# Two decoder layers on one core: two places for the stacks, four pairs of exponential tiles, and the last sums tile by tile

## The chip, the cores and the metric

The kernel runs on one core of one Trainium2 chip. The metric is the device time of one execution in microseconds (us). TensorE (PE in the rows), VectorE (DVE), ScalarE (ACT), GpSimd (POOL) and SyncE (SP) each run their own list of instructions in order and wait for one another through semaphores. SyncE issues every DMA of this kernel.

## The reference

Two transformer layers in float32 on x of 4 batches x 256 tokens x 256 features. A layer is attention and then a gated feed-forward part; each adds its input back and ends in a layer norm without weights.

```python
x = layernorm(x + attn0(x))   # 32 query heads of width 8, 8 key heads
x = layernorm(x + ffn0(x))    # weights rounded to fp8 e4m3, inner width 768
x = layernorm(x + attn1(x))   # 16 query heads of width 16, 8 key heads
x = layernorm(x + ffn1(x))    # weights = lut[idx], a table of 16 values, inner width 688
# attn: softmax(q k^T / sqrt(d)) v, then Wo;  ffn: down(silu(gate(x)) * up(x))
```

The weights of ffn0 are rounded to fp8 on the chip, and those of ffn1 are looked up on the chip from integer indices.

## The kernel before, in words

The work is cut into eight **jobs**: jobs 0 to 3 are layer 0 on batches 0 to 3, jobs 4 to 7 are layer 1 on the same batches. What each engine does, and in which order, is a table `ORDER` of five long lists of step names. `max.2.0` is step `max`, job 2, unit 0; a name on several engines is that engine's share of the same step. Matters go in steps like these:

- `q.j`, `kv.j`: projections on TensorE into one of three PSUM banks FB0 to FB2, then split by ScalarE and GpSimd into three bf16 parts (`QP`, `KP`).
- `qstack.j.part`, `kstack.j.part` on SyncE: 12 DMAs for a job (6 of `QP`, 6 of `KP`) that place the parts one above the other in the **stacks** `QS` and `KS`, from which TensorE computes float32-like scores with bf16 operands. A job's stacks lie in place `j % NST`; with `NST = 3` those of job j may be written when the scores of job j-3 are computed (`score_mm`).
- `max.j.u`: four matmuls into `MM` and one reduction on VectorE to the row maxima (`MX`). A job of layer 0 has 16 units, one of layer 1 has 8. The next unit's matmuls wait for the reduction of the one before, since there is one `MM`.
- `mt.j.p`: the negated maxima of half a job, turned by TensorE and sent by SyncE (`QS<-MP`) into two more rows of the stack. The scores of that half wait for it.
- `score.j.v`: scores less their maximum into `SC`, then the exponential on ScalarE into `PB`, a ring of `PB_QUADS = 3` pairs of tiles. `pv.*`: probabilities times values into `PV`; a pair is free when its `pv` are done (`pv_mm`).
- `stage`, `turn`, `back`, `wo`: normalise, turn back, output projection. `xadd`/`dsum` on GpSimd add to `X`, `wo`/`down` on VectorE take mean and variance, `wo`/`down` on GpSimd finish the layer norm; `tr.j.0`, `tr.j.1` turn `X` for the next product.
- `gu.j.i`, `hsplit.j.i`, `down.j.i`, i = 0 to 5: gate and up products, silu times up on VectorE (`HF`), its split by ScalarE (`HH`) and GpSimd (`HL`), and the down product.
- `q8.c` (12 pieces) make the fp8 weights, and `lutix.c`, `lutbits.c`, `lut1.c`, `lut2.c`, `lut3.c`, `lut4.c`, `lutlow.c` (10 pieces) those of layer 1: a binary selection from `LV`, of which there is one, so that `lut1` of a piece starts when `lutlow` of the one before has read it. `gu.0` waits for all of q8 and `gu.4` for all of the table.

At the end, ScalarE copies the last down product out of PSUM (L808), GpSimd adds it to `X` (L701), VectorE takes the statistics (L924, L929), GpSimd computes the norm (L653 to L657) and SyncE stores 256 KB (L610):

```python
pool.wait_ge(mv_done, n + 1)
pool.tensor_scalar(NM[:, n % 2, :], MV[:, n % 2, :, 0], -1.0, 0.0, ALU.mult, ALU.add)
link(pool.tensor_scalar(VE[:, n % 2, :], MV[:, n % 2, :, 1], 1.0, EPS, ALU.mult, ALU.add))
link(pool.tensor_tensor(RSTD[:, n % 2, :], VE[:, n % 2, :], NHALF[:, :], ALU.pow))
```

## Time and profile before

| | |
|---|---|
| time, median of 3 runs | 363.53 us (360.98 to 364.22) |
| the profiled execution | 362.06 us, its span 360.2 us |
| busy in the span | TensorE 83%, VectorE 72%, ScalarE 68%, GpSimd 54% |
| mean granted TensorE clock | 0.92 of full speed |

The span runs from the first to the last instruction of the profiled execution, and the 1.9 us of its time that are not in the span lie around it. Busy shares are means over stages that differ: VectorE has most of its work in the first 200 us and TensorE in the last 150.

### The profile page before, as it was taken

Reading aid. Unit: us, or ns where it says so; the run is one execution under the profiler, and the core shown is the slowest. Engines: PE = TensorE matmul, PEld = TensorE weight load, DVE = VectorE, ACT = ScalarE, POOL = GpSimd, SP = SyncE. Lnnn points to the kernel's source line nnn. Section 1 sums busy time; section 2 is a strip of 40 time slices with the busy share of each in tenths; the row PEclk is TensorE's granted clock in tenths of the full one; section 3 lists DMA queues with packets and bytes.
Section 4 is the critical chain, followed back from the end, with each engine's and each line's share of the span. In section 5 each row is a group of like instructions: output and inputs, shape, how many; then the busy total and the mean of one; then the engine's idle time right before and its main releaser. Section 6 shows DMA issues by size and latency. Waiting matters only on the chain.

```text
span 360.2 us, 7105 instructions
## 1 busy us (share of the span) xinstructions
PE 299.7 (83%) x2608; PEld 198.9 (55%) x2608; DVE 258.1 (72%) x399; ACT 246.3 (68%) x449; POOL 195.2 (54%) x261
## 2 busy tenths in 40 slices
PE   8446127687869897998979999999999999999990
PEld 7334002222426462564535765687778887979990
DVE  7695999898889897999986676656754657416341
ACT  3766677988588868797677776687677636654340
POOL 5756562404195348983398422564664346528763
PEclk9858555879899999999999999999999999999996
DMA  6468571201331000230001650032013000000000
GB/s 196 135 159 208 151 237 29 89 23 51 100 92 48 5 5 25 67 95 0 24 5 39 189 181 4 1 85 52 0 32 105 0 5 31 1 2 31 0 31 29
DMA packets 24872, 23.06 MB, mean 64 GB/s; under 512 B 3542, under 2 KB 24838, under 8 KB 24838
## 3 DMA queue, kind: packets, MB, share of 16 engines
q1 hardware_dynamic: 24838, 22.61, 22.2%
q8 instruction: 21, 0.34, 0.4%
q14 instruction: 13, 0.11, 0.1%
HBM read 10.47 MB, written 3.26 MB: 38 GB/s over the span
## 4 chain that ended last, share of the span: by engine, by line
PE 58%; DVE 13%; POOL 8%; ACT 8%; issue 7%; SPq 4%; DMA 2%; POOLq 0%; DVEq 0%; ACTq 0%
PE FB L1236 16%; PE PV L1179 9%; PE FB L1249 8%; PE MM L1124 6%; DVE LV L1042 5%; DVE MX L950 5%; PE SC L1158 4%; PE FB L1208 3%; PE SC L1153 2%; ACT PB L838 2%; PE FB L1078 2%; PE FB L1191 2%; SPq L542 2%; DMA QS<-QP 2%; ACT LV L885 2%
## 5 line engine op out<-in xcount | busy, mean ns | idle before, releaser
L950 DVE TENSOR_REDUCE MX<-MM 128x4 f32<-128x1024 f32 x96 | 117.0, 1219 | 40.1 <-PE MM L1124 39.5
L838 ACT ACTIVATE PB<-SC 128x1024 f32<-128x1024 f32 x96 | 98.2, 1023 | 31.7 <-PE SC L1153 19.5
L1124 PE MATMUL MM<-KS,QS 62*128 62x256 bf16 (+1 forms) x384 | 47.5, 292 | 33.6 <-DVE MX L950 24.8
L1179 PE MATMUL PV<-PB,VP 128*32 128x256 f32 x768 | 61.8, 408 | 1.3 <-ACT PB L838 1.3
L706 POOL TENSOR_TENSOR HL<-HF,HH 128x256 fp32r<-128x256 f32 (+1 forms) x48 | 37.6, 787 | 45.0 <-ACT HH L815 45.0
L1124 PEld LDWEIGHTS MM<-KS,QS 62*128 62x128 bf16 (+1 forms) x384 | 19.4, 97 | 59.4 <-DVE MX L950 39.4
L1042 DVE COPY_PREDICATED LV<-LB,LV 128x1728 f32<-128x1728 uint8 (+2 forms) x30 | 42.6, 1419 | 3.5 <-POOL LV L724 3.1
L1236 PE MATMUL FB<-XH,W 128*128 128x256 f32 x192 | 42.9, 305 | 0.5 <-DVE HF L1002 0.5
L1236 PE MATMUL FB<-XL,W 128*128 128x256 f32 x192 | 38.5, 282 | 0.0
L999 DVE SCALAR_TENSOR_TENSOR AA<-TH,FB 128x256 f32<-128x256 f32 (+1 forms) x48 | 20.0, 416 | 22.4 <-ACT TH L829 19.6
L1153 PE MATMUL SC<-QS,KS 64*128 64x256 bf16 x256 | 26.5, 287 | 9.8 <-ACT PB L838 7.8
L1236 PEld LDWEIGHTS FB<-XH,W 128*128 128x128 f32 x192 | 30.3, 190 | 6.5 <-issue 3.9
L1236 PEld LDWEIGHTS FB<-XL,W 128*128 128x128 f32 x192 | 29.5, 189 | 0.2 <-POOL XL L679 0.2
L1179 PEld LDWEIGHTS PV<-PB,VP 128*32 128x32 f32 x768 | 16.9, 110 | 22.6 <-issue 15.2
L724 POOL TENSOR_SCALAR LV<-LB,LD,LT 128x432 f32<-128x432 uint8 x40 | 28.1, 715 | 1.6 <-POOL LO L713 0.9
L885 ACT ACTIVATE LV<-LB,LT,LD 128x432 f32<-128x432 uint8 x40 | 27.4, 738 | 2.0 <-POOL LO L713 2.0
L657 POOL TENSOR_SCALAR X<-X,NM,RSTD 128x256 f32<-128x256 f32 x32 | 21.9, 693 | 1.7
L815 ACT ACTIVATE HH<-HF 128x256 fp32r<-128x256 f32 (+1 forms) x48 | 19.6, 412 | 4.6 <-DVE HF L1002 4.3
L1153 PEld LDWEIGHTS SC<-QS,KS 64*128 64x128 bf16 x256 | 8.9, 98 | 24.5 <-ACT PB L838 14.3
L1249 PE MATMUL FB<-W,HH 128*128 128x256 f32 (+1 forms) x96 | 22.0, 311 | 0.0
L664 POOL TENSOR_SCALAR W<-TH 128x384 fp32r<-128x384 f32 x12 | 6.9, 574 | 27.8 <-DVE TH L1019 27.8
L924 DVE BATCH_NORM_STATS2 BST<-X 128x6 f32<-128x256 f32 x32 | 11.9, 415 | 12.2 <-POOL X L701 11.9
(96 smaller groups left out, 578.5 us busy)
## 6 DMA issues: line engine op xcount, KB each, us to landing
QS<-QP SPq DMA_DIRECT2D x48, 128.0 KB, 2.4
IX<-in_idx SPq DMA_DIRECT2D x10, 216.0 KB, 4.0
dw<-LO SPq DMA_DIRECT2D x10, 216.0 KB, 2.1
W1L<-dw SPq DMA_DIRECT2D x10, 216.0 KB, 3.8
KS<-KP SPq DMA_DIRECT2D x24, 64.0 KB, 2.0
XT<-in_xt SPq DMA_DIRECT2D x4, 256.0 KB, 3.0
X<-in_x SPq DMA_DIRECT2D x4, 256.0 KB, 4.0
out<-X SPq DMA_DIRECT2D x4, 256.0 KB, 2.1
```

Source lines behind the costliest of these rows:

```text
L657: ins = pool.tensor_scalar(X[:, batch(j), t, :], X[:, batch(j), t, :], NM[:, n % 2, t:t + 1], RSTD[:, n % 2, t:t + 1], ALU.add, ALU.mult)
L706: pool.tensor_tensor(HL[0:r, i, :], HF[0:r, c % 2, :], HH[0:r, i, :].bitcast(F32), ALU.subtract).then_inc(h_parts, 1)
L724: ins = pool.tensor_scalar(LV[:, i, :], LB[:, 0, :], LD[:, i:i + 1], LT[:, 2 * i:2 * i + 1], ALU.mult, ALU.add)
L838: act.activation(PB[:, quad % PB_QUADS, kt, :, :], SC[:, :, :], ACT.Exp, scale=DH[layer(j)] ** -0.5).then_inc(exp_done, 1)
L885: ins = act.activation(LV[:, i, :], LB[:, 0, :], ACT.Identity, scale=LD[:, i:i + 1], bias=LT[:, 2 * i:2 * i + 1])
L950: dve.tensor_reduce(mx, MM[:, :, :].rearrange("p (f i) s -> p f i s", f=2), axis=AX.X, op=ALU.max).then_inc(max_red, 1)
L1042: ins = dve.copy_predicated(LV[:, 0:LUT // 2:2 * gap, :], mask, LV[:, gap:LUT // 2:2 * gap, :])
L1124: ins = pe.matmul(MM[:, 2 * f + i, :], QS[lo:lo + r, j % NST, qs + h, qt * P:(qt + 1) * P], keys(j)[lo:lo + r, j % NST, ks, :], start=True ...
L1153: ins = pe.matmul(SC[:, place(j, c), :], keys(j)[lo:lo + r, j % NST, ks, kt * P:(kt + 1) * P], QS[lo:lo + r, j % NST, qs + u % 4, :], star ...
L1179: ins = pe.matmul(PV[32 * c:32 * c + 32, r % 2, :], v, PB[:, quad % PB_QUADS, kt, place(j, c), :], start=part == 0, stop=part == (3, 1)[la ...
L1236: ins = pe.matmul(bank[:, w * S:(w + 1) * S], ffn_up(l, w, t, i)[part], xs[:, t, :], start=k == 0, stop=k == len(products) - 1)
L1249: ins = pe.matmul(bank[:, t * D:(t + 1) * D], hs[0:rows(l, i), i, t * P:(t + 1) * P], ffn_down(l, i)[part], start=i + k + t == 0, stop=(i, ...
```

## The change

The stacks have two places instead of three, so those of job j wait for the scores of job j-2; `QS`, `KS` and the value tiles shrink by a third, and so do the memsets at the start. The exponential tiles have four pairs instead of three. The norm's negated mean is no longer made; GpSimd subtracts the mean instead. In the last job the down product of each half of the tokens goes to a tile of its own in `MM`, VectorE adds it, takes the statistics and applies the norm, GpSimd only takes the power, and each half is stored by a DMA of its own. All five lists of `ORDER` are written anew. Each step is still there but for the last job's `down` on ScalarE and `dsum` on GpSimd, and VectorE has `fin` at its end.

```diff
-PB_QUADS = 3
+PB_QUADS = 4
 NFB = 3
-NST = 3
+NST = 2
...
     "PE": (
-        "q.0.0@0 q.0.1 kv.0.0@1 kv.0.1 kv.1.0@2 kv.1.1 q.1.0@0 q.1.1 max.0.0 q.2.0@1 q.2.1 q.3.0@0 q.3.1 max.0.1 "
+        "q.0.0@0 q.0.1 kv.0.0@1 kv.0.1 kv.1.0@2 kv.1.1 q.1.0@0 q.1.1 max.0.0 max.0.1 q.2.0@1 q.2.1 max.0.2 q.3.0@0 "
...
+                    if j == JOBS - 1:
+                        for t in range(TT):
+                            sp.wait_ge(x_last, t + 1)
+                            sp.dma_start(out[batch(j), t * P:(t + 1) * P, :], X[:, batch(j), t, :]).then_inc(out_wr, 16)
+                        continue
...
+                    if step == ("down", JOBS - 1):
+                        for t in range(TT):
+                            pool.wait_ge(var_last, t + 1)
+                            pool.tensor_tensor(RSTD[:, n % 2, t:t + 1], VE[:, n % 2, t:t + 1], NHALF[:, 0:1],
+                                               ALU.pow).then_inc(rstd_last, 1)
+                        continue
                     pool.wait_ge(mv_done, n + 1)
-                    pool.tensor_scalar(NM[:, n % 2, :], MV[:, n % 2, :, 0], -1.0, 0.0, ALU.mult, ALU.add)
...
-                        ins = pool.tensor_scalar(X[:, batch(j), t, :], X[:, batch(j), t, :], NM[:, n % 2, t:t + 1],
-                                                 RSTD[:, n % 2, t:t + 1], ALU.add, ALU.mult)
+                        ins = pool.tensor_scalar(X[:, batch(j), t, :], X[:, batch(j), t, :],
+                                                 MV[:, n % 2, t, 0:1], RSTD[:, n % 2, t:t + 1], ALU.subtract, ALU.mult)
...
+                    for t in range(TT):
+                        dve.wait_ge(down_half, t + 1)
+                        link(dve.tensor_tensor(X[:, b, t, :], X[:, b, t, :], MM[:, 2 * t, :], ALU.add))
+                        link(dve.bn_stats(BST[:, n % 2, t, :], X[:, b, t, :]))
+                        link(dve.bn_aggr(MV[:, n % 2, t, :], BST[:, n % 2, t, :]))
+                        dve.tensor_scalar(VE[:, n % 2, t:t + 1], MV[:, n % 2, t, 1:2], 1.0, EPS, ALU.mult,
+                                          ALU.add).then_inc(var_last, 1)
+                elif kind == "fin":
...
+                    for t in range(TT):
+                        dve.wait_ge(rstd_last, t + 1)
+                        dve.tensor_scalar(X[:, b, t, :], X[:, b, t, :], MV[:, n % 2, t, 0:1], RSTD[:, n % 2, t:t + 1],
+                                          ALU.subtract, ALU.mult).then_inc(x_last, 1)
...
+                    if j == JOBS - 1:
...
+                        for t in range(TT):
+                            for k, (part, hs) in enumerate(products):
+                                ins = pe.matmul(MM[:, 2 * t, :], hs[0:rows(l, i), i, t * P:(t + 1) * P],
+                                                ffn_down(l, i)[part], start=i + k == 0,
+                                                stop=(i, k) == (5, len(products) - 1))
+                            if i == 5:
+                                ins.then_inc(down_half, 1)
+                        continue
```

What the new lists do shows at three places. The line numbers of the changed kernel are higher by up to 49, so L1124 (the matmuls of `max`) is L1161 in it.

**TensorE at the start**, from `q.1` on. Before:

```order
L1078 MATMUL FB0<-XT,WQ0 128x256 x4
L1124 MATMUL MM<-KS,QS 128x256 x4
L1078 MATMUL FB1<-XT,WQ0 128x256 x4
L1078 MATMUL FB0<-XT,WQ0 128x256 x4
L1124 MATMUL MM<-KS,QS 128x256 x4
L1098 MATMUL FB2<-XT,WK0 64x256 x2
L1103 MATMUL FB2<-WV0,XT 128x64 x4
L1124 MATMUL MM<-KS,QS 128x256 x28
```

After:

```order
L1115 MATMUL FB0<-XT,WQ0 128x256 x4
L1161 MATMUL MM<-KS,QS 128x256 x8
L1115 MATMUL FB1<-XT,WQ0 128x256 x4
L1161 MATMUL MM<-KS,QS 128x256 x4
L1115 MATMUL FB0<-XT,WQ0 128x256 x4
L1161 MATMUL MM<-KS,QS 128x256 x4
L1135 MATMUL FB2<-XT,WK0 64x256 x2
L1140 MATMUL FB2<-WV0,XT 128x64 x4
L1161 MATMUL MM<-KS,QS 128x256 x20
```

The matmuls of `max.0.1` stood behind `q.2` and `q.3` and now stand ahead of both; `max.0.2` and `max.0.3` stand between `q.2`, `q.3` and `kv.2`.

**SyncE at the stacks of job 2**. `QS<-QP` and `KS<-KP` are the stacks' DMAs. Before:

```order
L542 DMA QS<-QP 16x8x512 [waits q_hi,stacks_set]
L542 DMA QS<-QP 16x8x512 x2
L521 DMA RAW<-in_up 128x384 [waits q8_used]
L542 DMA QS<-QP 16x8x512 [waits q_mid,stacks_set]
L542 DMA QS<-QP 16x8x512
L549 DMA KS<-KP 16x4x256 [waits k_hi,stacks_set]
L549 DMA KS<-KP 16x4x256 x2
L549 DMA KS<-KP 16x4x256 [waits k_mid,stacks_set]
L549 DMA KS<-KP 16x4x256
L542 DMA QS<-QP 16x8x512 [waits q_parts,stacks_set]
L549 DMA KS<-KP 16x4x256 [waits k_parts,stacks_set]
```

After (three of `QP`, behind the wait for `score_mm`, stand ahead of these rows):

```order
L545 DMA QS<-QP 16x8x512 [waits q_mid,score_mm,stacks_set]
L545 DMA QS<-QP 16x8x512
L552 DMA KS<-KP 16x4x256 [waits k_hi,score_mm,stacks_set]
L552 DMA KS<-KP 16x4x256 x2
L552 DMA KS<-KP 16x4x256 [waits k_mid,score_mm,stacks_set]
L552 DMA KS<-KP 16x4x256
L552 DMA KS<-KP 16x4x256 [waits k_parts,score_mm,stacks_set]
L588 DMA QS<-MP 2x8x256 [waits m_parts]
L588 DMA QS<-MP 2x8x256
L530 DMA IX<-in_idx 128x432 [waits ib_done]
L545 DMA QS<-QP 16x8x512 [waits q_parts,score_mm,stacks_set]
```

All twelve now wait for the last score of job 0, and the two DMAs `QS<-MP` of `mt.1.0`, for which the first score of job 1 waits, stand behind eleven of them.

**TensorE ahead of the first maxima of job 3** (`max.3.0`, the last row of both pieces). Before:

```order
L1098 MATMUL FB1<-XT,WK1 128x256 x2
L1179 MATMUL PV<-PB,VP0 32x256 x4
L1153 MATMUL SC<-QS,KS 128x256 x4
L1124 MATMUL MM<-KS,QS 128x256 x4
L1103 MATMUL FB1<-WV1,XT 128x128 x4
L1153 MATMUL SC<-QS,KS 128x256 x4
L1179 MATMUL PV<-PB,VP0 32x256 x4
L1217 MATMUL FB0<-IDN,X 128x128 x4
L1124 MATMUL MM<-KS,QS 128x256 x4
L1153 MATMUL SC<-QS,KS 128x256 x4
L1179 MATMUL PV<-PB,VP0 32x256 x4
L1124 MATMUL MM<-KS,QS 128x256 x4
```

After:

```order
L1273 MATMUL FB2<-XH,W0 128x256 x2
L1273 MATMUL FB2<-XL,W0 128x256 x2
L1161 MATMUL MM<-KS,QS 128x256 x4
L1245 MATMUL FB0<-WO0,ON 128x256 x2
L1190 MATMUL SC<-QS,KS 128x256 x4
L1216 MATMUL PV<-PB,VP0 32x256 x4
L1273 MATMUL FB0<-XH,W0 128x256 x2
L1273 MATMUL FB0<-XL,W0 128x256 x2
L1273 MATMUL FB0<-XH,W0 128x256 x2
L1273 MATMUL FB0<-XL,W0 128x256 x2
L1161 MATMUL MM<-KS,QS 128x256 x4
```

Before, `kv.4` (L1098, L1103) and `tr.1.0` (L1217) stand there, and `q.4` and all of job 0's feed-forward products further ahead. Now `gu.0.4` of job 0 (L1273) stands last ahead of `max.3.0`, and `q.4`, `kv.4`, `tr.0.1`, `tr.1.0`, `gu.0.5`, `down.0.3` to `down.0.5`, one `score` and one `pv` have moved behind it.

## Rows read from the trace of the kernel before

**Rows 1.** page, part 1: busy us, share of the span and count, by engine

```profile
PE 299.7 (83%) x2608; PEld 198.9 (55%) x2608; DVE 258.1 (72%) x399; ACT 246.3 (68%) x449; POOL 195.2 (54%) x261
```

**Rows 2.** stages: length, busy us (count) per engine, granted clock, DMA share

```profile
22.00:156.00 134.00, 97.34 (x876) 47.79 (x873) 117.25 (x144) 104.98 (x185) 71.79 (x89) 0.83 0.31 86
156.00:200.00 44.00, 38.85 (x375) 22.78 (x374) 36.99 (x53) 33.37 (x58) 29.15 (x34) 1.00 0.13 37
200.00:352.00 152.00, 151.61 (x1304) 118.83 (x1303) 86.81 (x179) 94.54 (x179) 78.03 (x112) 1.00 0.15 43
```

**Rows 3.** waits between 22 and 156 us: us in total, times, longest

```profile
DVE MX L950 <- PE MM L1124: 13.1, 16, 2.9
```

**Rows 4.** groups by line: busy us, mean ns, idle before and its releasers

```profile
L838 ACT ACTIVATE PB<-SC 128x1024 f32<-128x1024 f32 x96 | 98.2, 1023 | 31.7 <-PE SC L1153 19.5 <-PE SC L1158 10.8 <-PE PV L1179 1.1
```

**Rows 5.** the first maxima, in order of time: start us, length us

```profile
2.07 5.18 DVE L906 MEMSET QS<- 128x6144 uint32 x1 [2.07 <-issue]
...
21.63 0.61 PE L1124 MATMUL MM<-KS,QS 62*128 62x256 bf16 x4 [8.59 <-DMA KS<-KP]
...
22.28 1.23 DVE L950 TENSOR_REDUCE MX<-MM 128x4 f32<-128x1024 f32 x1 [0.31 <-PE MM L1124]
...
30.42 1.22 DVE L950 TENSOR_REDUCE MX<-MM 128x4 f32<-128x1024 f32 x1 [2.92 <-PE MM L1124]
```

**Rows 6.** SyncE's issues of the first job's stacks, in order of time

```profile
11.90 3.89 SPq L542 DMA_DIRECT2D QS<-QP  x6
...
16.52 3.71 SPq L549 DMA_DIRECT2D KS<-KP  x6
```

**Rows 7.** of the page, part 6: DMA issues, KB each, median us to landing

```profile
QS<-QP SPq DMA_DIRECT2D x48, 128.0 KB, 2.4
...
out<-X SPq DMA_DIRECT2D x4, 256.0 KB, 2.1
```

**Rows 8.** the first maxima of job 3 on VectorE

```profile
155.64 1.21 DVE L950 TENSOR_REDUCE MX<-MM 128x4 f32<-128x1024 f32 x1
```

**Rows 9.** pieces of the chain that ended last: start us, length us

```profile
201.95 0.48 PE FB L1236 x4
...
210.90 0.47 PE FB L1249 x4
...
233.13 0.86 PE FB L1078 x4
```

**Rows 10.** groups of the look-up table's chain, columns as in Rows 4

```profile
L724 POOL TENSOR_SCALAR LV<-LB,LD,LT 128x432 f32<-128x432 uint8 x40 | 28.1, 715 | 1.6 <-POOL LO L713 0.9 <-DVE LB L1027 0.7
...
L713 POOL TENSOR_TENSOR LO<-LV,W 128x432 f32<-128x432 f32 x10 | 11.6, 1165 | 14.4 <-ACT W L892 14.4
...
L892 ACT ACTIVATE W<-LV 128x432 fp32r<-128x432 f32 x10 | 5.6, 564 | 3.0 <-DVE LV L1042 3.0
...
L1042 DVE COPY_PREDICATED LV<-LB,LV 128x1728 f32<-128x1728 uint8 (+2 forms) x30 | 42.6, 1419 | 3.5 <-POOL LV L724 3.1
```

**Rows 11.** the end of the run, in order of time

```profile
348.20 0.41 DVE L999 SCALAR_TENSOR_TENSOR AA<-TH,FB 48x256 f32<-48x256 f32 x1
...
351.63 0.40 PE L1249 MATMUL FB<-W1L,HH 48*128 48x256 f32 x2
352.06 0.60 ACT L808 ACTIVATE RAW<-FB 128x512 f32<-128x512 f32 x1 [2.55 <-PE FB L1249]
352.74 1.26 POOL L701 TENSOR_TENSOR X<-X,RAW 128x512 f32<-128x512 f32 x1 [2.42 <-ACT RAW L808]
354.03 0.75 DVE L924 BATCH_NORM_STATS2 BST<-X 128x6 f32<-128x256 f32 x2 [4.97 <-POOL X L701]
354.82 0.25 DVE L929 BATCH_NORM_AGGREGATE MV<-BST 128x2 f32<-128x6 f32 x2
...
355.70 0.71 POOL L655 TENSOR_TENSOR RSTD<-VE,NHALF 128x2 f32<-128x2 f32 x1
...
357.64 0.37 SPq L610 DMA_DIRECT2D out<-X  x1
```

More of the change, by code:

```diff
@@ L345, in two_layer_kernel @@
         MV = sb("MV", [P, 2, TT, 2])
-        NM = sb("NM", [P, 2, TT])
         RSTD = sb("RSTD", [P, 2, TT])
@@ L412, in two_layer_kernel @@
         x_new = sem("x_new")
+        x_last = sem("x_last")
+        var_last = sem("var_last")
+        rstd_last = sem("rstd_last")
+        down_half = sem("down_half")
         th_done = sem("th_done")
@@ L611, in _ @@
                                  X[:, batch(j), :, :]).then_inc(out_wr, 16)
-            sp.wait_ge(out_wr, 16 * B)
+            sp.wait_ge(out_wr, 16 * (B + TT - 1))
         @block.gpsimd
@@ L804, in _ @@
                     j = step[1]
+                    if j == JOBS - 1:
+                        continue
                     act.wait_ge(down_ready, j + 1)
@@ L987, in _ @@
                     b = batch(j)
-                    dve.wait_ge(x_sum, j + 1)
-                    layer_norm(b, step)
+                    if j < JOBS - 1:
+                        dve.wait_ge(x_sum, j + 1)
+                        layer_norm(b, step)
+                        continue
+                    n = norms[step]
+                    dve.wait_ge(x_new, n - 1)
+                    for t in range(TT):
[6 more added lines that the diff above has]
+                elif kind == "fin":
+                    b = batch(JOBS - 1)
+                    n = norms["down", JOBS - 1]
+                    for t in range(TT):
+                        dve.wait_ge(rstd_last, t + 1)
+                        dve.tensor_scalar(X[:, b, t, :], X[:, b, t, :], MV[:, n % 2, t, 0:1], RSTD[:, n % 2, t:t + 1],
+                                          ALU.subtract, ALU.mult).then_inc(x_last, 1)
                 elif kind == "gu":
@@ L1246, in _ @@
                     products = ((0, HH), (0, HL), (1, HH))[:2 + l]
+                    if j == JOBS - 1:
+                        if i == 0:
+                            pe.wait_ge(max_red, unit0(JOBS))
+                        for t in range(TT):
[5 more added lines that the diff above has]
+                                ins.then_inc(down_half, 1)
+                        continue
                     for k, (part, hs) in enumerate(products):
```

236 rows, old and new, of the table ORDER are left out of this document.

## The prediction

> **What bounds the kernel now.** Begin with the busy shares [rows 1]: TensorE 83% and VectorE 72% leave open which of them sets the end, since both are means. The windows by stage tell it [rows 2]. From 200 to 352 us TensorE is busy 151.61 of 152 us, while VectorE has only 86.81: there the time is TensorE's work and nothing else. From 22 to 156 us VectorE is busy 117.25 of 134 and TensorE 97.34, at a granted clock of 0.83. This is VectorE's stage, with the reductions of `max`, the fp8 weights and the table. From 156 to 200 us both are near full (38.85 and 36.99 of 44). So the kernel is VectorE's work up to some point plus TensorE's work from that point on, and what I have to find is when the new order reaches that point, how much TensorE work is behind it, and how much idle time the two have. The first maxima of job 3 are a good point: VectorE reduces them at 155.64 us [rows 8], and the last matmul ends at 351.63 + 0.40 = 352.03 [rows 11]. Next read who is waited for. In VectorE's stage it waits 13.1 us in 16 pieces for the matmuls of `max` [rows 3], of its 134 - 117.25 = 16.75 idle us. ScalarE waited for a free pair of exponential tiles only once, 1.1 us of its 31.7 idle us before the exponential [rows 4].
>
> **Four pairs of tiles.** By themselves they are worth at most that 1.1 us, and ScalarE isn't what ends last; I count nothing. They let `pv` stand later in the order, and that goes with the order.
>
> **Two places for the stacks.** The memset of `QS` (5.18 us, [rows 5]) shrinks by a third, 1.7 us, and the two passes over `KS` with it. What is released last there is no memset: the first matmuls of `max` waited 8.59 us for the DMA of `KS` [rows 5], and `QP` is issued at 11.90 [rows 6], when its middle part is ready. I count nothing, between 0 and -1. The price of the change is the new wait. Twelve issues take 3.89 + 3.71 = 7.6 us and land 2.4 us later [rows 6, 7]: 10.0 us must lie between the last score of job j-2 and the first maxima of job j. By the durations of its steps TensorE has there 9.6, 15.8, 23.7, 10.4, 13.6 and 18.4 us for jobs 2 to 7 (for job 5: three `max` units, four `score`, three `pv`, two halves of `q.6`, one of `kv.6`, `wo`, `tr`, `turn`, `back`, the projections at 0.86 and the others near 0.5 each [rows 9]). Job 2 is short by 0.4, but VectorE has five reductions of 1.22 us and five table selections of 1.42 us in that stretch [rows 5, 10], 13.2 us, so this wait is covered; job 5 is covered by 0.4 if its K parts aren't late, and I give it 0 to 2 us, inside the idle time below. Queued behind the waiting issues on SyncE are the rows of `mt.1.0`. They go out after 11 issues (7 us) and land near 9.5; the first score of job 1 waits for them, with 8 us of VectorE work ahead of its next need.
>
> A rule of the Trainium skill bears on the stores below: DMA: Bandwidth & Descriptors, section on the anatomy of one DMA, says that about 2.0 us are fixed and the rest goes with bytes / 436e3. The trace agrees that the size counts for little: 128 KB land in 2.4 us and 256 KB in 2.1 [rows 7]. By the rule half the store would still gain 0.3 us; the rows show no gain, and the sum has none.
>
> **The order up to job 3's maxima.** I compared which steps stand ahead of `max.3.0`. On VectorE `gu.0.4`, `gu.0.5` and `down.0` have moved behind it (2 x 2 instructions of some 0.42, and 0.75 + 0.25: 2.7 us) and `lut2.8` ahead of it (the longest of three selections whose mean is 1.42, so near 2.2) [rows 10, 11]: -0.5. `lut3.0` now stands ahead of the first reduction, in a wait: -1.1. Waits: the second reduction came 8.1 us after the first with 2.92 us of waiting, because `q.2` and `q.3` stood between [rows 5]; now `max.0.1` is free of them. But `q.2` waits for an x tile that SyncE now loads two issues later. Between 0 and -2.9, I take -2. Of the other 10.2 us of waits for `max` I take 4 away (bounds 0 and 8), because TensorE has less to do in this stage, as the next part shows. A new wait: the table's chain from `lut4` to the next `lut2` is 0.56 + 1.17 + 4 x 0.715 = 4.6 us [rows 10], and between `lut4.4` and `lut2.5` VectorE has left only `lutbits.5` and two reductions, some 3.1 us (before there were a third reduction and the statistics of `wo.0`): +1.5. Together 155.6 - 1.6 - 2 - 4 + 1.5 = 149.5 us for job 3's first maxima.
>
> **TensorE from there on.** Before: 352.03 - 155.6 = 196.4, of which idle (44 - 38.85) + (152 - 151.61) = 5.5: 190.9 us of work. What has moved behind that point: `q.4` and `kv.4`, four halves of 0.86; `gu.0.5`, `tr.0.1` and `tr.1.0`, four times 0.48; three of `down.0`, 0.47 each; a `score` and a `pv`, together 1.0 [rows 9]: 3.4 + 1.9 + 1.4 + 1.0 = 7.8 us (rounded up by parts). So 198.7 us. This speaks against the new order: VectorE reaches the point earlier, but TensorE has more left. Between the first maxima of job 3 and those of job 4 there are now 47 us of TensorE work beside 38 of VectorE (before 40 beside 37), so TensorE becomes the bound a job earlier and should wait for VectorE less: idle 2.5 us in place of 5.5 (bounds 1 and 7). The last matmul then ends at 149.5 + 198.7 + 2.5 = 350.7.
>
> **The end.** Before, 360.2 - 352.03 = 8.15 us: copy 0.60, add 1.26, statistics 0.75 + 0.25, GpSimd's norm from there to 357.6, and 2.6 us from the store's issue at 357.64 to the end [rows 11]. Now, with VectorE: the first half is complete three matmuls before the end (-0.37). For each half an add (0.41, as L999), statistics 0.38, aggregation 0.13, the variance 0.1 (my estimate, from the aggregation) and four hand-overs of 0.04: 1.2 us. The second half is done 2.05 us after the last matmul, then the power 0.71 on GpSimd, the norm on VectorE (no row for it; between the 0.38 of the statistics and the 0.71 of the power, 0.42 as L999) and with hand-overs 3.3; store and landing 2.6: 5.9 us. That is -2.25, bounds -1.5 and -2.8. The dropped negated mean takes one small instruction out of each of GpSimd's other norms, which I count at nothing.
>
> **The sum.** 350.7 + 5.9 = 356.6 us of span, and 1.9 around it: 358.5 against the profiled 362.06, a fall of 3.6. The profiled execution lies 1.5 under the median of 363.53 and 1.1 over the fastest; I set the fall against the mean of all four times, 362.7: **359.1 us**.
>
> **The rivals.**
> 1. Only the end gains. The 4 us of waits stay, as VectorE's waits come from `max` standing one unit behind a `score` or `pv` and not from how much TensorE has to do: the middle gives back what it gains, and 362.7 - 2.3 = 360.4, or 361 with the table's wait. For it: many waits are pieces of 0.4 to 0.8 us (13.1 in 16). Against: the 7.8 us.
> 2. The order removes nearly all waits of VectorE's stage: 8 us in place of 4 and idle time of 1.5 behind it: 354. For it: 16.75 us idle is a lot. Against: the new wait of the table and the narrow stacks.
> 3. Slower: the stacks come late. Place: SyncE's queue at jobs 2, 5 and 6, where the twelve issues have 10 to 14 us. If ScalarE's and GpSimd's splits of K follow the last exponential by more than the 7.6 us of issues, each such job stops TensorE, and with it everything behind the blocked `QS<-MP`; 3 us at each of three jobs turn 359.1 into 368. It decides for slower than before where the stacks and their blocked queue cost more than 3.6 us in all.
> 4. The change does not do what it says: the four pairs aren't used, since ScalarE hardly waited for one [rows 4]. Then the time is that of rival 1.
>
> **How the numbers follow.** Forecast 0.42; rivals 1 and 4 together 0.28; rival 2 0.19; rival 3 0.11. One per cent, 3.6 us, is about what a measurement of this kernel tells from no change. Faster by over that (under 359.9): two thirds of the forecast's spread, all of rival 2 and a little of rival 1, 0.51. Slower (over 367.2): most of rival 3, 0.08. Between: 0.41. Range 353.5 to 365.5: the forecast with its bounds (-4 and +4.5), rivals 1 and 2, and the lower part of rival 3; behind its ends are some 0.2.
>
> **What would show it.** In the new profile: job 3's first maxima near 149.5 us; the wait for `max` in VectorE's stage at 5 to 8 us; a wait of 1 to 2 us at `LV` near 95 us; TensorE full from about 155 us on, with under 4 us of idle time to its end; the last matmul 5.9 us ahead of the end of the span. I am wrong if the first maxima of jobs 2, 5 or 6 wait for a DMA of the stacks, if the first maxima of job 3 come after 153 us, or if TensorE still waits over 5 us behind them.

## The result, and the profile after

The changed kernel takes **375.9 us** (median of 4, 375.35 to 376.21) where the kernel before, timed beside it, took 363.3 us (360.98 to 364.22): ratio 1.0355, interval 1.0305 to 1.0406. It is 3.5% slower. The forecast was 359.1 us with a range to 365.5, so even the range missed. The ratios and intervals below leave out the few executions that lie over 1.5% above the fastest of their kernel; medians hold all of them.

The profiled execution took 375.77 us, its span 373.8. The busy shares of the page:

```profile
PE 313.0 (84%) x2608; PEld 201.2 (54%) x2608; DVE 257.1 (69%) x405; ACT 249.1 (67%) x448; POOL 204.9 (55%) x242
```

Against [rows 1], TensorE is busy 13.3 us longer with the same 2608 matmuls, and GpSimd 9.7 us longer with 19 instructions fewer. These are the first two signs: neither engine has more to do, each takes longer for it. The stages, with the granted clock behind the busy times:

```profile
22.00:156.00 134.00, 100.62 (x826) 44.11 (x826) 117.40 (x138) 101.60 (x174) 62.77 (x76) 0.73 0.28 83
156.00:200.00 44.00, 38.56 (x354) 24.00 (x352) 33.30 (x52) 30.73 (x56) 34.41 (x37) 1.00 0.25 73
200.00:365.00 165.00, 158.22 (x1354) 120.44 (x1355) 91.35 (x184) 103.19 (x192) 93.61 (x107) 1.00 0.12 32
```

In [rows 2] the first stage had 876 matmuls in 97.34 us at a clock of 0.83. Now there are 50 fewer of them in 3.3 us more, at 0.73. From 200 us on TensorE was idle 0.4 us; now it idles 6.8 of 165. The chain that ended last, by engine and by line, and GpSimd's norm among the groups:

```profile
PE 45%; POOL 21%; DVE 9%; ACT 8%; issue 7%; SPq 6%; DMA 2%; POOLq 0%; ACTq 0%; DVEq 0%
PE FB L1273 10%; POOL X L671 9%; PE PV L1216 8%; PE FB L1298 6%; PE MM L1161 5%; DVE MX L968 4%; PE SC L1190 4%; ACT PB L856 3%; POOL RSTD L669 3%; PE SC L1195 2%; PE FB L1245 2%; PE FB L1254 2%; SPq L552 2%; SPq L545 2%; POOL HL L722 2%
...
L671 POOL TENSOR_SCALAR X<-X,MV,RSTD 128x256 f32<-128x256 f32 x30 | 40.1, 1344 | 1.6
```

L671 is the line that subtracts the mean and multiplies. Its mean is 1344 ns. The row of the kernel before that answers to it, which the prediction never looked at, reads:

```profile
L657 POOL TENSOR_SCALAR X<-X,NM,RSTD 128x256 f32<-128x256 f32 x32 | 21.9, 693 | 1.7
```

The same tile, the same engine, twice the time. `tr`, TensorE's step behind each norm, waits for it; first the changed kernel's waits, then those of the kernel before (us in total, times, longest):

```profile
PE FB L1254 <- POOL X L671: 7.8, 9, 1.4
```

```profile
PE FB L1217 <- POOL X L657: 1.7, 3, 0.8
```

Job 3's first maxima, and the end of the run in order of time:

```profile
154.21 1.22 DVE L968 TENSOR_REDUCE MX<-MM 128x4 f32<-128x1024 f32 x1
```

```profile
368.00 0.28 PE L1290 MATMUL MM<-W1L,HH 48*128 48x256 f32 x1
368.03 0.42 DVE L1014 TENSOR_TENSOR X<-X,MM 128x256 f32<-128x256 f32 x1 [2.69 <-PE MM L1290]
...
369.69 0.43 DVE L1015 BATCH_NORM_STATS2 BST<-X 128x6 f32<-128x256 f32 x1
370.15 0.18 DVE L1016 BATCH_NORM_AGGREGATE MV<-BST 128x2 f32<-128x6 f32 x1
370.36 0.15 DVE L1017 TENSOR_SCALAR VE<-MV 128x1 f32<-128x1 f32 x1
...
370.60 0.66 POOL L664 TENSOR_TENSOR RSTD<-VE,NHALF 128x1 f32<-128x1 f32 x1 [0.62 <-DVE VE L1017]
370.87 1.21 SPq L615 DMA_DIRECT2D out<-X  x2
371.29 0.41 DVE L1025 TENSOR_SCALAR X<-X,MV,RSTD 128x256 f32<-128x256 f32 x1 [0.45 <-POOL RSTD L664]
```

Job 3's maxima came at 154.2, not at 149.5. The end is as forecast: 5.5 us from the last matmul (368.28) to the end of the span, where the kernel before had 8.15. Note L1025: VectorE does the same subtract-and-multiply in 0.41 us.

### The profile page after: what moved, and what is told of

Its sections match the earlier page's. It is cut to its first block, busy times and chain, and to the rows that moved or that the text cites. A ratio compares the mean times of both kernels' runs of the same rounds, so it can differ in the third digit from the quotient of the medians.

```text
span 373.8 us, 7087 instructions
## 1 busy us (share of the span) xinstructions
PE 313.0 (84%) x2608; PEld 201.2 (54%) x2608; DVE 257.1 (69%) x405; ACT 249.1 (67%) x448; POOL 204.9 (55%) x242
## 4 chain that ended last, share of the span: by engine, by line
PE 45%; POOL 21%; DVE 9%; ACT 8%; issue 7%; SPq 6%; DMA 2%; POOLq 0%; ACTq 0%; DVEq 0%
PE FB L1273 10%; POOL X L671 9%; PE PV L1216 8%; PE FB L1298 6%; PE MM L1161 5%; DVE MX L968 4%; PE SC L1190 4%; ACT PB L856 3%; POOL RSTD L669 3%; PE SC L1195 2%; PE FB L1245 2%; PE FB L1254 2%; SPq L552 2%; SPq L545 2%; POOL HL L722 2%
## 5 line engine op out<-in xcount | busy, mean ns | idle before, releaser
L1161 PE MATMUL MM<-KS,QS 62*128 62x256 bf16 (+1 forms) x384 | 49.8, 307 | 29.0 <-DVE MX L968 20.3
L1216 PE MATMUL PV<-PB,VP 128*32 128x256 f32 x768 | 64.9, 426 | 2.8 <-ACT PB L856 2.8
L722 POOL TENSOR_TENSOR HL<-HF,HH 128x256 fp32r<-128x256 f32 (+1 forms) x48 | 35.1, 738 | 41.0 <-ACT HH L833 41.0
L1161 PEld LDWEIGHTS MM<-KS,QS 62*128 62x128 bf16 (+1 forms) x384 | 19.5, 100 | 57.5 <-DVE MX L968 34.2
L1079 DVE COPY_PREDICATED LV<-LB,LV 128x1728 f32<-128x1728 uint8 (+2 forms) x30 | 41.2, 1374 | 6.9 <-POOL LV L740 5.8
L1273 PE MATMUL FB<-XH,W 128*128 128x256 f32 x192 | 43.3, 307 | 1.4 <-DVE HF L1039 1.4
L671 POOL TENSOR_SCALAR X<-X,MV,RSTD 128x256 f32<-128x256 f32 x30 | 40.1, 1344 | 1.6
L1273 PE MATMUL FB<-XL,W 128*128 128x256 f32 x192 | 39.0, 285 | 0.0
L1273 PEld LDWEIGHTS FB<-XH,W 128*128 128x128 f32 x192 | 30.3, 192 | 9.2 <-issue 5.2
L1190 PE MATMUL SC<-QS,KS 64*128 64x256 bf16 x256 | 28.5, 306 | 5.6 <-ACT PB L856 4.7
L1216 PEld LDWEIGHTS PV<-PB,VP 128*32 128x32 f32 x768 | 17.2, 113 | 26.7 <-issue 16.9
L1273 PEld LDWEIGHTS FB<-XL,W 128*128 128x128 f32 x192 | 30.0, 192 | 0.4 <-POOL XL L693 0.2
L740 POOL TENSOR_SCALAR LV<-LB,LD,LT 128x432 f32<-128x432 uint8 x40 | 28.4, 720 | 1.3 <-POOL LO L729 0.7
L729 POOL TENSOR_TENSOR LO<-LV,W 128x432 f32<-128x432 f32 x10 | 11.2, 1123 | 21.2 <-ACT W L910 21.2
L1298 PE MATMUL FB<-W,HH 128*128 128x256 f32 (+1 forms) x84 | 19.5, 313 | 0.4 <-POOL HL L722 0.4
```

The lines of the kernel that those rows point to most:

```text
L671: ins = pool.tensor_scalar(X[:, batch(j), t, :], X[:, batch(j), t, :], MV[:, n % 2, t, 0:1], RSTD[:, n % 2, t:t + 1], ALU.subtract, ALU.mult)
L722: pool.tensor_tensor(HL[0:r, i, :], HF[0:r, c % 2, :], HH[0:r, i, :].bitcast(F32), ALU.subtract).then_inc(h_parts, 1)
L740: ins = pool.tensor_scalar(LV[:, i, :], LB[:, 0, :], LD[:, i:i + 1], LT[:, 2 * i:2 * i + 1], ALU.mult, ALU.add)
L1079: ins = dve.copy_predicated(LV[:, 0:LUT // 2:2 * gap, :], mask, LV[:, gap:LUT // 2:2 * gap, :])
L1161: ins = pe.matmul(MM[:, 2 * f + i, :], QS[lo:lo + r, j % NST, qs + h, qt * P:(qt + 1) * P], keys(j)[lo:lo + r, j % NST, ks, :], start=True ...
L1190: ins = pe.matmul(SC[:, place(j, c), :], keys(j)[lo:lo + r, j % NST, ks, kt * P:(kt + 1) * P], QS[lo:lo + r, j % NST, qs + u % 4, :], star ...
```

## The experiments

Each group of kernels was timed beside the kernel before on a chip of its own: experiments 1 to 4, 5 and 6, 7 and 8, and 9. The median of the kernel before was 363.4, 362.0, 362.6 and 361.9 us in them. Between groups I compare ratios, and a difference of a few tenths of a per cent between groups is not resolved. The first three kernels take the change apart.

**1. new_negmean: the changed kernel with the old form of the norm.**

```diff
+pool.tensor_scalar(NM[:, n % 2, :], MV[:, n % 2, :, 0], -1.0, 0.0, ALU.mult, ALU.add)
...
-MV[:, n % 2, t, 0:1], RSTD[:, n % 2, t:t + 1], ALU.subtract, ALU.mult)
+NM[:, n % 2, t:t + 1], RSTD[:, n % 2, t:t + 1], ALU.add, ALU.mult)
```

> The changed kernel, with the norm on GpSimd as before: the negated mean is made again, and the norm adds it (add, multiply) where the change subtracts the mean (subtract, multiply). Orders, places, tile pairs and the last job's end stay those of the change. Theory A (the subtracting form is slow on GpSimd: 1344 ns mean in the profile after, 693 before, two in each of 15 norms, and the norms lie on the path): the norms fall back to some 0.69 us each, 9 to 13 us go, and the time is 360 to 366 us. Theory B (the two places of the stacks and the new order are what costs, and the long norms mostly fill gaps): at least 370 us.

Measured 367.0 us (365.6 to 368.2), ratio 1.0103 [1.0066, 1.0139]. The norm's form costs 8.9 us in the new order; without it the kernel is still 1% slower than before, in spite of the faster end.

**2. old_submean: the kernel before with the new form of the norm**, the same three lines the other way round, one instruction fewer in each norm.

> The kernel before, with one edit: the norm on GpSimd subtracts the mean, and the negated mean is not made. Theory A: the norm's tensor_scalar takes 1.2 to 1.35 us in place of 0.69, and the time goes up by 5 to 12 us, to 368 to 375 us. Theory B: under 2 us, to at most 365 us, because in the old order the norms have slack.

Measured 375.2 us (374.3 to 377.3), ratio 1.0338 [1.0298, 1.0379]: just over the upper end of what was expected. This one edit costs 11.8 us in the old order, nearly as much as the whole change. Its groups and waits have the same two rows as the changed kernel:

```profile
L656 POOL TENSOR_SCALAR X<-X,MV,RSTD 128x256 f32<-128x256 f32 x32 | 45.9, 1441 | 1.7
```

```profile
PE FB L1216 <- POOL X L656: 9.1, 6, 3.2
```

**3. old_newend: the kernel before with the new end of the last job**, and nothing else of the change.

```diff
+dve.wait_ge(down_half, t + 1)
+link(dve.tensor_tensor(X[:, b, t, :], X[:, b, t, :], MM[:, 2 * t, :], ALU.add))
...
+ins = pe.matmul(MM[:, 2 * t, :], hs[0:rows(l, i), i, t * P:(t + 1) * P],
```

> The kernel before, with the last job's end of the change alone (down product by halves into MM, sums, statistics and norm on VectorE, power on GpSimd, two stores); the other norms stay as before. By the working of the prediction the end after the last matmul falls from 8.15 to 5.9 us and the time by 2 to 2.5 us, to about 361 us. Rival: the two stores and the hand-overs take it back, and the time stays within 1 us of 363.3.

Measured 359.6 us (358.3 to 360.5), ratio 0.9891 [0.9853, 0.9930]: 3.9 us faster than the kernel before, more than the 2.3 of the forecast's term. In the profiled executions the end itself is 2.65 us shorter (8.15 to 5.5), which lies just inside the interval of the ratio (2.5 to 5.3 us).

**4. forms: what in the instruction costs the time.** The kernel before with 28 `tensor_scalar` of 128 x 256 float32 on GpSimd behind its last norm, four of each form; it computes something into a tile that nobody reads.

> The kernel before, with 28 linked tensor_scalar instructions at the end of GpSimd's list, each on 128x256 float32 from scratch to scratch, four of each form: (1) add NM, multiply RSTD; (2) subtract NM, multiply RSTD; (3) add MV, multiply RSTD; (4) subtract MV, multiply RSTD; (5) subtract MV alone; (6) add NM alone; (7) multiply RSTD, add NM. If the operation is what costs, (2), (4) and (5) take some 1.2 us and (1), (3), (6), (7) some 0.55. If the place of the scalar (MV in place of NM) is what costs, (3), (4) and (5) are slow. If it is neither but the company of VectorE, all seven take the same here.

One execution, 387.0 us; the forms are compared within it. The rows are start, length of four, and the tiles; in the order of the rows the operations are add and multiply (L730), subtract and multiply (L732), the same two with the mean read from `MV` (L734, L736), subtract alone (L738), add alone (L740), multiply and add (L742).

```profile
358.31 2.51 POOL L730 TENSOR_SCALAR XF<-WF,NM,RSTD 128x256 f32<-128x256 f32 x4
360.93 5.18 POOL L732 TENSOR_SCALAR XF<-WF,NM,RSTD 128x256 f32<-128x256 f32 x4
366.21 2.51 POOL L734 TENSOR_SCALAR XF<-WF,MV,RSTD 128x256 f32<-128x256 f32 x4
368.82 5.17 POOL L736 TENSOR_SCALAR XF<-WF,MV,RSTD 128x256 f32<-128x256 f32 x4
374.09 3.97 POOL L738 TENSOR_SCALAR XF<-WF,MV 128x256 f32<-128x256 f32 x4
378.16 3.98 POOL L740 TENSOR_SCALAR XF<-WF,NM 128x256 f32<-128x256 f32 x4
382.24 2.51 POOL L742 TENSOR_SCALAR XF<-WF,RSTD,NM 128x256 f32<-128x256 f32 x4
```

It is the operation, not the place of the scalar: subtract in the first of the two places takes 1.29 us where add takes 0.63, whether the mean comes from `NM` or with its stride from `MV`. The form with one operation takes 0.99 us either way, which was not expected (1.2 for subtract, 0.55 for add): what doubles the time is subtract ahead of a second operation. Subtract in the second place was not run. So the cheap way to subtract here is to negate a small tile once and add it.

The next kernels look for the other 7.5 us, between new_negmean (367.0) and old_newend (359.6). These two have the same norm and the same end; they differ in the order, the two places and the four pairs.

**5. new_nst3 and new_pb3: the places and the pairs.** new_pb3 is new_negmean with `PB_QUADS = 3`. new_nst3 has `NST = 3` as well, with `ones.6` ahead of `kstack.5.0` on SyncE.

> The changed kernel with the negated mean and the add-and-multiply norm back (new_negmean, 367.0 us), and in it three places for the stacks and three pairs of exponential tiles again; only ones.6 moves in SyncE's list, ahead of kstack.5.0, since place 0 is another now. The order stays the new one. If the narrow stacks hold SyncE, ScalarE and TensorE up (ScalarE waited 5.5 us for QS<-QP, job 2), this gives back most of the 7.5 us between new_negmean and old_newend: 360 to 363. If the order itself is at fault (TensorE at half its clock until 110 us, and the moved work behind it): 365 to 369, within 1% of new_negmean.

> new_negmean with three pairs of exponential tiles in place of four, and nothing else. The prediction counted nothing for the fourth pair, since ScalarE had waited 1.1 us for one in the kernel before. If the new order uses the fourth pair (its pv stand later), this is slower: 369 to 373. If not: 366 to 368.

Timed side by side, new_pb3 has a ratio of 1.0111 [1.0072, 1.0150] (366.6 us) and new_nst3 of 1.0069 [1.0025, 1.0112] (366.0 us). The fourth pair is worth nothing that shows, as forecast (1.0111 without it, 1.0103 with it, each good to 0.4%). The two places cost 1.5 us by the ratios and 0.6 by the medians; the intervals overlap, so anything from nothing to some 3.5 us fits. So the order itself holds most of the 7.5 us.

new_nst3 showed something else. The nine executions in its ratio span 5.4 us, and they line up with their mean granted clock: 361.5 and 361.6 us at 0.915 and 0.918, 364.1 at 0.903, and six of 365.1 to 366.9 at 0.890 to 0.898. The kernel before stayed at 0.915 to 0.925 beside them. The same instructions in the same order took 4 to 5 us less in the two executions with the high clock. Whether the clock made these short, or both follow from the waits falling differently, this doesn't show.

**Where the clock is low.** The windows have their bounds at VectorE's reductions: first maxima of job 0, ninth of job 0, ninth of job 1, first of job 2, first of job 3, last matmul. First old_newend, then new_negmean:

```profile
23.00:51.00 28.00, 11.52 (x60) 6.68 (x60) 22.35 (x25) 19.42 (x41) 17.71 (x21) 0.62 0.77 194
51.00:88.10 37.10, 25.18 (x250) 8.24 (x250) 33.70 (x44) 30.94 (x52) 11.55 (x17) 0.81 0.22 72
88.10:110.00 21.90, 16.20 (x160) 7.18 (x160) 19.06 (x23) 17.12 (x28) 11.64 (x16) 0.92 0.30 85
110.00:156.30 46.30, 41.54 (x404) 24.23 (x400) 42.27 (x54) 36.98 (x65) 30.18 (x35) 1.00 0.11 32
156.30:352.60 196.30, 190.73 (x1680) 141.87 (x1678) 124.39 (x233) 128.13 (x237) 107.09 (x147) 1.00 0.14 41
```

```profile
22.20:47.00 24.80, 12.69 (x60) 7.10 (x60) 21.51 (x22) 15.11 (x29) 15.22 (x18) 0.64 0.54 159
47.00:87.50 40.50, 30.14 (x238) 9.73 (x238) 34.61 (x44) 30.94 (x53) 10.04 (x17) 0.61 0.19 57
87.50:110.60 23.10, 17.61 (x128) 6.88 (x128) 19.88 (x21) 17.30 (x31) 9.73 (x13) 0.63 0.39 111
110.60:154.10 43.50, 36.72 (x380) 18.74 (x379) 41.30 (x53) 37.75 (x61) 24.55 (x30) 1.00 0.17 51
154.10:359.20 205.10, 200.82 (x1746) 148.64 (x1744) 127.78 (x240) 134.41 (x248) 114.81 (x159) 1.00 0.15 42
```

Read each line pair. The new order wins the first stretch: 24.8 against 28.0 us. It loses the second (40.5 against 37.1) and the third (23.1 against 21.9), where the clock is 0.61 and 0.63 against 0.81 and 0.92, that is mostly at 1.2 GHz and not at 2.4. There 366 matmuls take 30.14 + 17.61 = 47.75 us, 130 ns each; in the old order 410 take 25.18 + 16.20 = 41.38, 101 ns each. At the old order's pace the 366 would take 36.9, so the low clock costs TensorE 10.8 us in this stretch. That the two orders have other matmuls there doesn't explain it: the 96 matmuls of `max` that stand in both are busy 13.1 us against 10.5, and those of `pv`, busy time over count, 117 ns each against 93. By line, new_negmean from 47.0 to 110.6 us:

```profile
L1218 PE MATMUL PV<-PB,VP 128*32 128x256 f32 x152 | 17.8, 555 | 2.0 <-ACT PB L858 2.0
L1163 PE MATMUL MM<-KS,QS 62*128 62x256 bf16 x96 | 13.1, 366 | 8.0 <-DVE MX L970 7.8
```

and old_newend from 51.0 to 110.0 us:

```profile
L1217 PE MATMUL PV<-PB,VP 128*32 128x256 f32 x176 | 16.4, 450 | 0.4 <-ACT PB L857 0.3
L1162 PE MATMUL MM<-KS,QS 62*128 62x256 bf16 x96 | 10.5, 301 | 7.5 <-DVE MX L969 7.3
```

But these 10.8 us are TensorE's, and the stage is VectorE's. The new order loses 4.6 us of time in the two stretches; 1.7 of them are more work of VectorE there (54.49 us against 52.76), and only 2.9 are idle time of VectorE, which is all that a slow TensorE can have cost.

The new order gains the fourth stretch (43.5 against 46.3) and then has 200.82 us of matmuls behind job 3's maxima against 190.73. All in all it has 68 matmuls fewer ahead of that point and 10 us more of them behind it, and is busy 2.7 us longer ahead of it all the same.

**6. new_rep_score and new_rep_both: the same matmuls issued twice**, to keep TensorE busier there (the results stay the same). new_rep_both also issues the last matmul of `max` twice, from unit 8 of job 0 to the end of job 2.

```diff
-for c in range(4):
+for c in (0, 1, 2, 3, 2, 3) if j <= 1 else range(4):
...
+for c in (0, 1, 2, 3, 3) if j <= 1 else range(4):
...
+for i, f in ((0, 0), (0, 1), (1, 0), (1, 1)) + ((1, 1),) * (8 <= m < 48):
```

The first added line is new_rep_score's, the other two are new_rep_both's.

> new_negmean in which two of the four matmuls of each score of jobs 0 and 1 are issued twice (64 matmuls more, the same results into the same places): work without use, which keeps TensorE busier between 47 and 110 us, where the trace of new_negmean shows half the clock in nearly every stretch of 5 us and that of old_newend the full one from 65 us. If idle time of TensorE is what keeps the clock down and the low clock is what costs the lead, the full clock comes earlier, and the time falls to 361 to 365 in spite of 10 to 20 us of added work. If the clock is only a companion, the added work costs: 368 to 374.

> As new_rep_score, but one matmul repeated in each score of jobs 0 and 1 and one in each max from unit 8 of job 0 to unit 15 of job 2 (72 more). The added matmul of max stands in VectorE's chain (0.2 us or less each at full clock, 0.3 to 0.4 at half). By the clock's theory 361 to 366; by the other 370 to 380, since some 12 us come into the chain.

Ratios 1.0112 [1.0039, 1.0185] and 1.0135 [1.0079, 1.0192]; the medians of all four executions are 368.0 and 370.6 us, their ranges 363.7 to 370.0 and 366.7 to 373.2. Neither gets faster; by the ratios neither pays for the added work in full. The one trace of new_rep_both, its fastest execution, shows what happens, with bounds at the same reductions:

```profile
45.50:83.70 38.20, 27.15 (x268) 11.29 (x268) 34.90 (x44) 32.27 (x55) 10.74 (x18) 0.83 0.20 62
83.70:107.70 24.00, 19.46 (x143) 8.74 (x143) 19.75 (x19) 17.47 (x31) 9.64 (x12) 0.64 0.37 105
107.70:154.20 46.50, 42.37 (x408) 22.07 (x405) 41.35 (x53) 37.84 (x61) 24.19 (x30) 0.93 0.17 48
```

From the ninth maxima of job 0 to those of job 1 it issues 30 matmuls more than new_negmean and takes 38.2 us instead of 40.5, at a clock of 0.83 instead of 0.61; with the 1.5 us that it was ahead before, it stands 3.8 us ahead there (83.7 against 87.5). Behind that the clock is at 0.64 again, and job 3's maxima come at 154.2, where they came without the added work. VectorE's idle time in the first of these stretches is 3.3 us where new_negmean has 5.9. So in this trace a higher clock and a lead came together in one stretch; I did not find a way to hold it.

**7. old_warm and new_warm: added matmuls ahead of the stretch**, six into the score tile ahead of each of eight waits for `max`, in old_newend and in new_negmean.

```diff
+if 1 <= m <= 8:
+    for _ in range(6):
+        pe.matmul(SC[:, 0, :], QS[0:r, 0, 0, 0:P], keys(0)[0:r, 0, 0, :], start=True, stop=True)
```

> old_newend with six more matmuls (work without use, into the score tile before its first use) ahead of each of eight waits for max, units 1 to 8 of job 0, 25 to 52 us. There the granted clock is 0.50 from 36 to 65 us and TensorE idle 70 to 80%. If idle time keeps the clock down, it rises 10 to 25 us earlier and the waits for max in this stretch shrink: 356 to 359. If the added work only stands in the way: 360 to 365.

> new_negmean (367.0) with the same added matmuls. Its clock stays at 0.50 for most of the stretch to 110 us. If it is a matter of how the clock enters the stretch, it falls to 360 to 364; if the clock falls again behind the added work because the order leaves TensorE idle then, the time stays within 1% of new_negmean, 365 to 369.

Medians 361.9 and 368.9 us, ratios 0.9981 [0.9957, 1.0005] against 0.9891 for old_newend, and 1.0121 [1.0081, 1.0161] against 1.0103. Neither gains; the old one loses 2 to 3 us. In old_warm the clock from 23 to 40 us is higher than in old_newend (0.80 against 0.70), but from 40 to 60 us it is at 0.50 in both, with TensorE busy 5.39 and 5.11 of each 10 us in old_warm, and then lower than in old_newend (0.84 against 0.92 from 60 to 90). So added matmuls are no tool for it here. What either order would take if it entered the stretch at the full clock stays untested, since no kernel did.

**8. hyb_early and hyb_mid: the new order up to a point, the old one from there**, three places and three pairs, the new end.

Each engine's list is the new one up to a step and then what is left of the old one in its own order; `mt.0.1` keeps the new one's bank. Shown is the seam of TensorE's list in hyb_early, where `-` is the new order's line and `+` the hybrid's:

```diff
 score.0.5 pv.0.1.0
-max.1.0 mt.0.1@1 pv.0.1.1 score.0.6 max.1.1 max.1.2
+score.0.6 pv.0.1.1 max.1.0 mt.0.1@1 max.1.1 score.0.7
```

In hyb_early the other engines leave the new list ahead of `max.1.0` (VectorE), `score.0.6` (ScalarE), `q8w.9` (GpSimd) and `ldix.6` (SyncE); in hyb_mid ahead of `max.2.0` (TensorE and VectorE), `score.1.4`, `lut1.6.0` and `mt.1.1`.

> old_newend (359.6 us; three places, three pairs, the new end) with the new order up to the first maxima of job 1 and the old order from there on (the lists of the changed kernel up to that point on each engine, then what is left of the old lists in their own order). The new order reaches job 1 at 65.1 us, the old one at 69.9, the new one with one fp8 piece less done. If the lead is lost only because the new order goes on as it does, it stays here: 355 to 357. If it is lost to whatever follows (waits for max that come with the lead): 359 to 361, as old_newend.

> The same, with the new order up to the first maxima of job 2 (110 us in both orders) and the old one from there on. If the 7.5 us between new_negmean and old_newend lie behind that point (more TensorE work behind job 3's maxima, 200.8 against 190.7 us), this is back at 359 to 361. If they are work that the new order has not done by that point, it stays at 363 to 367.

Medians 368.7 and 380.7 us, ratios 1.0170 [1.0133, 1.0207] and 1.0510 [1.0461, 1.0559]. Both expectations fail, since each hybrid has a stall of its own at the seam: in hyb_early VectorE waits 10.6 us for an fp8 piece on ScalarE, in hyb_mid a score waits 10.4 us for the rows of `mt`. Their first halves say nothing. What stands behind the seam does: from job 1's ninth maxima hyb_early needs 264.5 us to the last matmul (95.7 to 360.2), as old_newend does (88.1 to 352.6), and from job 3's first maxima hyb_mid reads

```profile
179.20:375.50 196.30, 190.73 (x1680) 141.88 (x1678) 124.41 (x233) 128.14 (x237) 107.12 (x147) 1.00 0.14 41
```

which is old_newend's last window again, to 0.01 us of TensorE's work. With the new order it is 205.1 us, and 205.1 to 205.3 in each variant of it that has the old norm. So what comes behind job 3's maxima is set by what the order left for it, and in none of these kernels did anything ahead of that point change it. It also says where the new order loses: of the 6.7 us between the profiled executions of new_negmean and old_newend (364.8 and 358.1), 8.8 are lost behind job 3's maxima and 2.2 gained ahead of them. The new order would have to reach them some 9 us earlier than the old one to break even, and it is 2.2 earlier.

**9. old_max01: the start alone.** One move in old_newend's list: the second unit of `max` ahead of `q.2` and `q.3`.

```diff
-max.0.0 q.2.0@1 q.2.1 q.3.0@0 q.3.1 max.0.1
+max.0.0 max.0.1 q.2.0@1 q.2.1 q.3.0@0 q.3.1
```

> old_newend (359.6 us) with one move in TensorE's list alone: the second unit of max stands ahead of q.2 and q.3, as in the new order. The forecast took 2 us (bounds 0 and 2.9) for this. In the trace of new_negmean VectorE waited 2.3 us less than in old_newend between the first and the ninth maxima (3.3 against 5.6). If that is what this move gives and nothing behind takes it back: 357.5 to 358.5. If the waits come back later at a lower clock or behind other steps, as the whole new order gave its lead back by job 1: 359 to 360.5.

Measured 359.6 us (12 executions), ratio 0.9942 [0.9920, 0.9965]. The same median as old_newend; its ratio is rather worse than old_newend's 0.9891 [0.9853, 0.9930], but that was measured on another chip and the intervals overlap. All that can be said is that no gain shows. VectorE has 0.9 us less from the first to the ninth maxima, and all of it is gone by job 1's ninth, at 88.1 us in both:

```profile
23.10:50.20 27.10, 11.25 (x60) 6.36 (x60) 22.43 (x26) 19.39 (x41) 17.99 (x23) 0.63 0.76 202
50.20:88.10 37.90, 26.50 (x250) 8.68 (x250) 33.79 (x43) 30.96 (x52) 11.46 (x17) 0.76 0.21 69
```

Again the second stretch takes longer at a lower clock (0.76 against 0.81) with the same 250 matmuls, and one new wait of 0.98 us at 79.0 us for a unit of `max` that stands behind a score.

**The best version** is the kernel before with the new end, old_newend: 359.6 us, 1.1% faster than before, its interval wholly below 1. With old_max01, which has the same end and gained 0.6% in more executions on another chip, 0.6 to 1.1% is what the new end can be said to be worth.

## Why the prediction was wrong

The time: 375.9 measured, 359.1 forecast. In spans of profiled executions the 17.2 us between 356.6 and 373.8 divide like this, with new_negmean as the step between:

| step of the prediction | forecast | measured | off by |
|---|---|---|---|
| the norm without the negated mean | 0 | 373.8 - 364.8 | +9.0 |
| job 3's first maxima | 149.5 | 154.1 | +4.6 |
| TensorE's work behind them | 198.7 | 200.8 | +2.1 |
| its idle time behind them | 2.5 | 205.1 - 200.8 = 4.3 | +1.8 |
| from the last matmul to the end | 5.9 | 364.8 - 359.2 = 5.6 | -0.3 |

**The step that failed** is "the dropped negated mean takes one small instruction out of each of GpSimd's other norms, which I count at nothing". I counted the instruction that went and overlooked the operation that changed in the one that stayed: add became subtract, on 30 tiles. Its price is 30 x (1.344 - 0.693) = 19.5 us of GpSimd, of which 8.9 us reach the end in the new order and 11.8 in the old. No row of the kernel before shows a subtract of this form on GpSimd, so its price was unknown, and where the prediction bounded other unknown prices from both sides, it put this one at nothing. It also decides why the idle time behind job 3's maxima is 12.2 us in the changed kernel (214.1 us, of which TensorE is busy 201.9) and 4.3 without it: each norm stands between GpSimd and `tr`, for which TensorE waits 7.4 us there, and 0.3 in new_negmean.

It is not the only step that failed: new_negmean, without this cost, took 367.0 us, still above the range's 365.5. The second is the 4 us taken off the waits for `max` (below); with the work moved behind job 3's maxima, it turned the forecast gain into a loss of 1%. Two of the prediction's three signs of being wrong came: job 3's first maxima after 153 us (154.2), and TensorE waiting over 5 us behind them (12.2). The third, a stop at the stacks, did not.

**Four pairs: nothing.** Right as far as it can be told, ratio 1.0103 with and 1.0111 without.

**Two places: 0 to 2 us, covered; the memset nothing.** About right: the first maxima came at 22.2 us against 23.0 in old_newend and 22.3 before, and the places cost 0 to 3.5 us. TensorE waited for no stack of jobs 2, 5 or 6. What I had not seen is that ScalarE waits more for `QS<-QP`, 5.5 us ahead of job 3's maxima in new_negmean against 2.2 in old_newend: the stacks of job 2 go out late, and `QP` is not free for the next split. Rival 3 (stacks late, 368) has the right direction and is close in number to new_negmean, but its mechanism, a stop of TensorE at the stacks, isn't there.

**The order up to job 3's maxima: -6.1 us.** Measured from old_newend it is -2.2 (156.3 to 154.1), by the windows of experiment 5: -0.8 ahead of the first maxima, -0.1 of VectorE's work behind them (I had -1.6 with `lut3.0`), -1.3 of its idle time (I had -4.5). Right at the start, wrong behind it. The waits at the start shrank by 2.3 us, where I took 2. Of the 4 us that I took from the other waits nothing came: VectorE idles 14.6 us from its first maxima to those of job 3, where old_newend idles 15.9, so 1.1 us came back of what the start gave. The new wait of the table didn't come: VectorE waited 1.0 us at `LV` where old_newend waited 2.0 and the kernel before 0.3, and I had added 1.5. The wait for `max` in the stage, for which I had named 5 to 8 us as the sign, is 11.7 in 14 pieces in the changed kernel (13.1 in [rows 3]). I argued that TensorE "has less to do in this stage" and would be waited for less. It had less to do, and it did that at 0.61 and 0.63 of its clock and needed more time for it: from 47.0 to 110.6 us VectorE idles 9.1 us, where old_newend idles 6.2 from 51 to 110. Rival 1 had the right doubt, that the waits don't depend on how much TensorE has to do.

**TensorE from there on.** Right in kind, short in size: 7.8 us moved by my list, 10.1 in the traces. Counted in both traces, 66 matmuls more stand behind the point, where my list makes 60: the other 6 are most of a step of `gu`. The lists didn't move it. TensorE runs ahead of VectorE at this point, and it had the matmuls of `max.3.0` done 2.3 us ahead of their reduction in old_newend (153.97 and 156.3) and 1.5 us in new_negmean (152.6 and 154.1), so the old order had more done by then. That is 0.8 us; the other 1.5 are the prices of the moved steps, which I took too low, and aren't split further. That TensorE would idle less there was right, without the norm's cost: 4.3 us against 5.6, where I had 2.5.

**The end: 5.9 us.** Right: 5.5 in the changed kernel, by the same pieces. Adds 0.42, statistics 0.43, aggregation 0.18, variance 0.15, power 0.66, norm 0.41, as costed within 0.1 each. From the end of the last norm (371.70) to the end of the span are 2.1 us where [rows 11] had 2.6, so half the store did gain some 0.4. The rule that the prediction set aside, of the Trainium skill's page DMA: Bandwidth & Descriptors (anatomy of one DMA), by which half the bytes save 0.3, was nearer than my zero. The page gives it for DMAs issued by GpSimd, and here SyncE issues them, so the agreement is this one number.

**What stays open.** That TensorE's work takes longer at the low clock is measured. That this is what makes VectorE wait in the early stretch of the new order is argued, from the windows, from new_nst3's executions and from one stretch of new_rep_both; at most 2.9 us of time hang on it in the profiled execution. Which steps of the order bring the clock down wasn't shown: added matmuls raised it only in part, and both hybrids were spoiled by their seams. The plain rival is the 10 us of matmuls moved behind job 3's maxima, which cost 8.8 us there, and the new lists with those steps put back ahead were not run.

## What to carry to other kernels

When a change replaces an instruction by a "simpler" one, price the one that stays by its exact operations, from a row that has them; where no row has them, that edit has a range and not a zero. Work moved off a stage that another engine bounds is not saved: here 2.2 us came back ahead and 8.8 were paid where TensorE is the bound. And fewer matmuls were not less time here, since they ran at a lower clock: read the granted clock beside the busy time. And take a change apart before you judge it: this one held a gain of 1.1% beside losses of 2.5% (the norm's form) and 2.1% (the order and the places).

## What the runs showed of the hardware

- On GpSimd a `tensor_scalar` of 128 x 256 float32 with two operations takes 0.63 us with add or multiply first and 1.29 us with subtract first; the form with one operation takes 0.99 us with either add or subtract (forms). On VectorE subtract and multiply takes 0.41 us (the changed kernel's end). GPSIMD Engine Reference of the Trainium skill (engine selection) calls GpSimd "roughly line-rate" for elementwise work with one input; here it is 1.5 times VectorE's time in its best form and 3.1 times with subtract.
- The same kernel on the same chip took 361.5 us in an execution with a mean granted clock of 0.915 and 366.9 in one with 0.894, with no change in its instructions (new_nst3).
- A busy TensorE isn't a TensorE at full clock: in new_negmean it was busy 8.09 us between 70 and 80 us at a granted clock of 0.50, and in old_newend 6.28 us in the same ten at 1.00.
- Issuing matmuls twice went with less time in one stretch of one trace: 30 more came with 38.2 us in place of 40.5, the clock at 0.83 in place of 0.61 (new_rep_both). The whole kernel didn't gain.
